# Starting the large on-chip buffers of a four-stage transformer layer at multiples of 128 bytes

## The reference, cut to what matters

```python
# 1  "cond": nine gated experts (eight weighted by gating probabilities, one shared), all on every token
out1 = (1 - sg) * sum_e g[e] * ((silu(x @ Wg[e]) * (x @ Wu[e])) @ Wd[e]) + sg * shared(x)     # 256 -> 1024 -> 256
# 2  "hyp": causal attention, 16 heads of 16, with hyperbolic distances as scores, then a projection
# 3  "cond2": two dense shared networks relu(x @ swi) @ swo, and one chosen by the sequence's type (5 types),
#            weighted by a small softmax gate
# 4  "ffn": layernorm, a 3-tap convolution, causal rotary attention, layernorm, a router (argmax over 4 experts)
#            and out = x + (silu(h @ wv_gate) * (h @ wv_value)) @ proj of the chosen expert, 256 -> 1024 -> 256
```

## The kernel before, in words

| stage | moving operand | loaded operand |
|---|---|---|
| cond up, B11, B21, B22, T1 | `cond_x_hi_first` 16512 (128) | `cond_w_hi` 123776 (128), `cond_w_lo` 152448 (128) |
| cond up, T2, T3, T4; remainders | `cond_x_hi` 82816 (128), `cond_x_lo` 95104 (128) | the same |
| cond down | `cond_h_hi` 197504 (128), `cond_h_lo` 205696 (128) | `cond_d_hi` 181120 (128), `cond_d_lo` 189312 (128) |
| hyp projection | `hyp_wq_hi` 64384 (128), `hyp_wq_lo` 70528 (128) | `hyp_src_hi` 152512 (192), `hyp_src_lo` 160704 (192) |
| dense up | `c_x_hi` 141728 (160), `c_x_lo` 158112 (160) | `dense_w_hi` 177696 (32), `dense_w_lo` 185888 (32) |
| dense down | `dense_h_hi` 210464 (32), `dense_h_lo` 218656 (32) | `dense_d_hi` 194080 (32), `dense_d_lo` 202272 (32) |
| typed up | `typed_x_hi` 158112 (160), `typed_x_lo` 162208 (160) | `typed_w_hi` 125344 (160), `typed_w_lo` 133536 (160) |
| rope projection | `rope_wq_hi` 221152 (224), `rope_wq_lo` 215008 (224) | `rope_src_hi` 156800 (128), `rope_src_lo` 164992 (128) |
| moe up | `moe_x_hi` 165152 (32), `moe_x_lo` 169248 (32) | `moe_w_hi` 116000 (32), `moe_w_lo` 132384 (32) |

## Time and profile before

### The profile page before, as it was taken

How to read it: one execution, slowest core, us unless ns; L and a number is a source line. 1 busy time by engine, 2 the same in 40 slices (tenths; PEclk the granted TensorE clock), 3 DMA queues, 4 the chain that set the end, 5 groups by cost and what they waited for, 6 DMA issues and landing times. The chain is left out here.

```text
span 2069.8 us, 35351 instructions
## 1 busy us (share of the span) xinstructions
PE 1923.5 (93%) x12240; PEld 1620.3 (78%) x12240; DVE 1434.9 (69%) x2398; ACT 1105.4 (53%) x2118; POOL 849.8 (41%) x854
## 2 busy tenths in 40 slices
PE   8999999999999999999998677999999768959998
PEld 6788888888888888888887465788799646849998
DVE  7777676767767676776776896433589577857776
ACT  6555555545555554555544697232355365636664
POOL 7350321405032140504200185220399225968885
PEclk9999999999999999999999799999999779969999
DMA  4101010010101001010102201310156215556661
GB/s 155 62 1 62 1 61 0 20 41 0 61 0 61 0 23 37 0 61 0 29 1 62 62 3 42 123 41 11 63 192 211 65 26 148 185 204 209 213 214 45
DMA packets 96322, 144.51 MB, mean 70 GB/s; under 512 B 15358, under 2 KB 72608, under 8 KB 96096
## 3 DMA queue, kind: packets, MB, share of 16 engines
q1 hardware_dynamic: 89168, 127.21, 19.1%
q0 software_dynamic: 4928, 12.86, 1.8%
q10 hardware_dynamic: 2128, 3.15, 0.4%
HBM read 111.46 MB, written 14.16 MB: 61 GB/s over the span
## 5 line engine op out<-in xcount | busy, mean ns | idle before, releaser
L319 PE MATMUL ps<-cond_x_lo,cond_w_hi 128*128 128x512 f32 x1008 | 392.6, 389 | 0.0
L471 ACT ACTIVATE cond_h_hi<-cond_h 128x512 fp32r<-128x512 f32 x288 | 174.0, 630 | 289.7 <-DVE cond_h L666 289.6
L805 POOL TENSOR_TENSOR cond_w_lo<-cond_stage_up,cond_w_hi 128x512 fp32r<-128x512 f32 x36 | 47.1, 1308 | 591.8 <-ACT cond_w_hi L471 591.8
L319 PE MATMUL ps<-cond_x_hi_first,cond_w_hi 128*128 128x512 f32 x578 | 230.1, 398 | 3.1 <-DVE ps L652 2.5
L382 PE MATMUL ps<-cond_h_hi,cond_d_hi 128*128 128x512 f32 x576 | 224.8, 390 | 4.1 <-DVE cond_h_lo L671 4.1
L319 PE MATMUL ps<-cond_x_hi_first,cond_w_lo 128*128 128x512 f32 x578 | 225.2, 390 | 0.0
L382 PE MATMUL ps<-cond_h_hi,cond_d_lo 128*128 128x512 f32 x576 | 224.3, 389 | 0.0
L382 PE MATMUL ps<-cond_h_lo,cond_d_hi 128*128 128x512 f32 x576 | 224.2, 389 | 0.0
L319 PEld LDWEIGHTS ps<-cond_x_lo,cond_w_hi 128*128 128x128 f32 x1008 | 189.3, 188 | 37.2
L649 DVE TENSOR_TENSOR ps<-cond_p_row,ps 128x512 f32<-128x512 f32 x142 | 98.7, 695 | 170.7 <-PE ps L319 170.7
L524 ACT ACTIVATE cond_h<-ps 128x512 f32<-128x512 f32 x216 | 124.7, 596 | 164.8 <-DVE cond_h_lo L671 132.2
(11 more groups left out here) (427 smaller groups left out, 5122.4 us busy)
## 6 DMA issues: line engine op xcount, KB each, us to landing
moe_stage_up<-in_L_ffn_expert_wv SPq DMA_DIRECT2D x22, 1024.0 KB, 7.9
typed_stage_up<-in_L_cond_wi SPq DMA_DIRECT2D x11, 1024.0 KB, 5.0
typed_stage_dn<-in_L_cond_wo SPq DMA_DIRECT2D x11, 1024.0 KB
moe_stage_dn<-in_L_ffn_expert_proj SPq DMA_DIRECT2D x11, 1024.0 KB
cond_stage_up<-in_L_cond_Wg SPq DMA_DIRECT2D x7, 1024.0 KB, 5.1
cond_stage_up<-in_L_cond_Wu SPq DMA_DIRECT2D x7, 1024.0 KB, 7.2
cond_stage_dn<-in_L_cond_Wd SPq DMA_DIRECT2D x7, 1024.0 KB, 9.5
rope_v_now<-rope_v_blk SPq DMA_DIRECT2D x16, 272.0 KB, 2.4
```

What stands on the lines that cost most here:

```text
L319: ins = pe.matmul(bank, ws[:, j, u, w], xs.rearrange("p o n -> p (o n)"), start=(opens and k == 0), stop=(k == 2), skip_group_check=True)
L471: copy = lambda dst, src: act.activation(dst, src, ACT.Copy)
L805: return pool.tensor_tensor(w_lo[:, j, :, A11:A12 + 1], raw_up[:, :, :, upper(j)], w_hi[:, j, :, A11:A12 + 1], ALU.subtract)
```

## The change

A helper `fill_line` allocates an unused buffer just large enough that the next buffer starts at a multiple of 128 bytes, and it is called ahead of the large buffers of each stage. `spike` and `space` are split over two lines for it, and in `rotary` the two buffers `v_now` and `yT` change places. No instruction is added, removed or moved; what differs is the addresses in them.

```diff
--- before.py
+++ after.py
@@ -28,6 +28,7 @@
 E_COND, E_TYPE, E_SHARED, E_MOE = 8, 5, 2, 4
 SLOT = 256
 HEAD = 2
+LINE = 128
 
 SLOTS = max((N + E_TYPE * (SLOT - T)) // SLOT, (N + E_MOE * (SLOT - 1)) // SLOT)
 LN_EPS = 1e-5
@@ -77,6 +78,13 @@
 
 def aligned(at):
     return (at + 31) // 32 * 32
+
+
+def fill_line(nc, ctx, side=None):
+
+    short = nc.sbuf_top % LINE if side else -aligned(nc.sbuf_base) % LINE
+    if short:
+        ctx.enter_context(nc.sbuf_tensor(f"fill_{aligned(nc.sbuf_base)}", [P, short // 4], F32, side=side))
 
 
 class StageSemaphores:
@@ -961,6 +969,7 @@
 
     with ExitStack() as s:
         sb = lambda name, shape, dt=F32: s.enter_context(nc.sbuf_tensor(f"{tag}_{name}", shape, dt))
+        fill_line(nc, s)
         w_hi = sb("w_hi", [P, ups, KC, F], F32R)
         w_lo = sb("w_lo", [P, ups, KC, F], F32R)
         d_hi = sb("d_hi", [P, FC, D], F32R)
@@ -1261,6 +1270,7 @@
         self.m, self.biased = m, b_qkv is not None
         if b_qkv is not None:
             self.bias, self.bo, self.ws = sb("bias", [P, 2 * D]), sb("bo", [P, KC]), sb("ws", [P, KC])
+            fill_line(nc, ctx, side)
             self.vb = sb("vb", [P, D])
             self.loads += [(self.bo[:], col(b_out)), (self.ws[:], col(w_sur)),
                            (self.vb[:], b_qkv[2 * D:].unsqueeze(0).to_broadcast([P, D]))]
@@ -1309,8 +1319,10 @@
         wide = lambda v: v.unsqueeze(0).to_broadcast([P, D])
         self.loads = [(self.w[:], wide(ln_w)), (self.b[:], wide(ln_b)), (self.wr[:], w_r.rearrange("(k p) e -> p k e", p=P))]
         self.loaded = ctx.enter_context(nc.semaphore("router_loaded"))
+        fill_line(nc, ctx)
         self.res, self.x = sb("res", [P, 2, KC, P]), sb("x", [P, 2, D])
         self.stats, self.mean, self.rstd = sb("stats", [P, 2, 6]), sb("mean", [P, 2, 2]), sb("rstd", [P, 2])
+        fill_line(nc, ctx)
         self.x2, self.xn, self.rows, self.hT = sb("x2", [P, 2, D]), sb("xn", [P, 2, D]), sb("rows", [P, 2, 2 * D]), sb("hT", [P, 2, KC, P])
         self.eps, self.logits = sb("eps", [P, 1]), sb("logits", [P, NP, E_MOE])
         self.best, self.free, self.hot = sb("best", [P, NP]), sb("free", [P, NP]), sb("hot", [P, NP, E_MOE])
@@ -1622,7 +1634,9 @@
         v_blk = sb("v_blk", [P, NP, 2, HP, 2, VW])
         wo = w.wo
         bias, bo, ws = w.bias, w.bo, w.ws
-        spike, space = sb("spike", [P, NP]), sb("space", [P, NP, 2 * H])
+        spike = sb("spike", [P, NP])
+        fill_line(nc, s)
+        space = sb("space", [P, NP, 2 * H])
 
         sem = StageSemaphores(nc, tag + "_in")
         src_rounded, src_ready = sem("src_rounded"), sem("src_ready")
@@ -1638,6 +1652,7 @@
             src_hi, src_lo = sb1("src_hi", [P, 2, KC, TW], F32R), sb1("src_lo", [P, 2, KC, TW], F32R)
             v_row, v_two = sb1("v_row", [P, 2, SUB, D]), sb1("v_two", [P, 2, SUB, 2, D])
             sig = sb1("sig", [P, NP])
+            fill_line(nc, s1)
             sq = sb1("sq", [P, 2, QK])
             r2, ln, root, inv, ep, en, sm, ser, below, cosh = (
                 sb1(n, [P, NP, 2 * H]) for n in ("r2", "ln", "root", "inv", "ep", "en", "sm", "ser", "below", "cosh"))
@@ -1907,13 +1922,14 @@
     chosen, last_steps, last_lifted = sem("chosen"), sem("last_steps"), sem("last_lifted")
     with ExitStack() as s:
         sb = lambda name, shape, dt=F32: s.enter_context(nc.sbuf_tensor(f"{tag}_{name}", shape, dt))
+        fill_line(nc, s)
         qk, v_blk = sb("qk", [P, NP, QK]), sb("v_blk", [P, NP, 2, HP, 2, VW])
         wo, wq_hi, wq_lo = w.wo, w.wq_hi, w.wq_lo
         hi_at = aligned(nc.sbuf_base)
         src_hi, src_lo = sb("src_hi", [P, 2, KC, TW], F32R), sb("src_lo", [P, 2, KC, TW], F32R)
         v_row, v_two = sb("v_row", [P, 2, SUB, D]), sb("v_two", [P, 2, SUB, 2, D])
         x32, rot = sb("x32", [P, 2, QK]), sb("rot", [P, 2, QK])
-        v_now, yT = sb("v_now", [P, 2, 2, HP, 2, VW]), sb("yT", [P, 2, KC, P])
+        yT, v_now = sb("yT", [P, 2, KC, P]), sb("v_now", [P, 2, 2, HP, 2, VW])
         mx, rec = sb("mx", [P, 2, H]), sb("rec", [P, 2, H])
 
         def placed(at, *parts):
@@ -2989,6 +3007,7 @@
     dn_half_done = sem("dn_half_done")
     with ExitStack() as s_:
         sb = lambda name, shape, dt=F32: s_.enter_context(nc.sbuf_tensor(f"{tag}_{name}", shape, dt))
+        fill_line(nc, s_)
         w_hi, w_lo = sb("w_hi", [P, ups, KC, F], F32R), sb("w_lo", [P, ups, KC, F], F32R)
         d_hi, d_lo = sb("d_hi", [P, FC, D], F32R), sb("d_lo", [P, FC, D], F32R)
         x_hi, x_lo = sb("x_hi", [P, 2, KC, SLOT], F32R), sb("x_lo", [P, 2, KC, SLOT], F32R)
@@ -3454,6 +3476,7 @@
                     ffn(nc, m, "dense", False, groups, None, [s0, s1], x_hi, x_lo, stage, SortBeside(lists, rows, slots))
                     sem.give_back()
                 brief = right.enter_context(ExitStack())
+                fill_line(nc, right, "right")
                 rope = AttentionWeights(nc, m, right, brief, "rope", a["L0_ffn_attn_w"], a["L0_ffn_proj_w"], side="right")
                 joining = JoinWeights(nc, brief, a["L0_cond2_g1"], a["L0_cond2_g2"], a["L0_ffn_ln1_w"], a["L0_ffn_ln1_b"],
                                       a["L0_ffn_conv_w"])
```

## The result

The changed kernel takes 2078.88 us (median of 5 runs, 2075.32 to 2079.67), the kernel before 2066.95 (5 runs beside them, 2065.03 to 2069.87): 11.9 us more, ratio 1.005, 95% interval 1.0039 to 1.0062. It is slower, as forecast, by three quarters of the 16 us that were forecast; 2083 lay 4 us above the measured time.

The account below looks back on a forecast made before the run. PE was taken to bound the kernel, its matmuls covering 93% of the span and all of cond; +17 us in cond and -0.6 in rope, +16 on the median 2066.95, gave 2083 us, range 2061 to 2091.

Parts of the forecast that it names:

- Reading (b): TensorE's pace depends on the distance by 256 between moving operand and weights; slower, 2083 us (2072 to 2091), chance 0.48.
- Reading (a): TensorE's pace depends on absolute starts: those that are not multiples of 128 cost time.
- rival 3: Stages outside cond get faster from multiples of 128: about 2063 us (chance 0.12) or 2045 (0.08), 0.20 together.
- Rival 2: No change: TensorE's pace doesn't depend on starts; 2067 us, 2064 to 2070, chance 0.32.
- rival 4: Cond's buffers were aligned already, so the change has no effect there; same time as no change, no chance of its own.
- The price of a disturbed matmul: Cond: 12 matmuls of each group of 33 slow to dense up's pace, +5.0 ns each, 60 ns a group.
- The price of healing: Cond: three matmuls behind each of three disturbed runs lose 6.6 ns each, 59 ns a group.
- The parts priced at nothing: Hyp, dense, typed, moe, ACT, POOL, DVE and DMA: 0 us each, some with small bounds.
- point ii: Sign in the profile after: dense up still at 232 ns between starts.
- point iv: Sign in the profile after: moe and typed at 120.0 ns between starts.
- Point (i): Sign: cond's settled matmuls at about 230 ns instead of 226.7, about 434 in 100 us, cond ending 15 us later.
- point iii: Rope's 512-column projection settles at 226.7 ns as its distance goes from 160 to 0; -0.6 us over 96 matmuls.

Follow-up runs that it names:

- i_cond_all128: Kernel before with 128 unused bytes between cond's token-side operands and its weights, putting all 21 up matmuls of a group at distance 128: 2085.93 us, ratio 1.0082.
- a_cond_shift: Kernel before with 128 unused bytes ahead of cond's own buffers, `cond_x_hi_first` not moved: 2079.02 us, ratio 1.0044.
- b_after_cond_back: Changed kernel with 128 more unused bytes ahead of cond's own buffers, bringing `cond_x_hi_first` back to distance 0: 2067.76 us, ratio 0.9992 to the kernel before.
- c_all_160: Kernel before with 160 unused bytes below everything, `cond_x_hi_first` included, no distance within a stage changed but rope's: 2070.66 us, ratio 1.0004.
- first scan: Kernel before with unused bytes ahead of dense weights (128), typed and moe token operands (128, 64) and hyp's source (192): 2064.28 us, ratio 0.9973.

## Why the prediction was right, and where its working was not

**The mechanism.** Reading (b) stands: the distance between the moving operand and the weights loaded beside it. Moving the loaded operand (`i_cond_all128`), or both but `cond_x_hi_first` (`a_cond_shift`), brings the loss; distance 0 at other absolute starts (`b_after_cond_back`, `c_all_160`) is free of it. Reading (a), rival 3, is out by the same two runs, and by dense, which the change aligned and left at 1.39 us for 6. Rival 2, no dependence on starts, and rival 4, that the change does nothing in cond, are out by `a_cond_shift`. Why a distance should matter is not settled by any run; that the two reads of TensorE meet in one part of the memory in some order that depends on it fits, but it is argued, not shown. The rule of the Trainium skill (SBUF — State Buffer, Who interferes with whom) that TensorE's two read ports are independent and that it waits on nobody does not hold for the pace here: moving one operand by 128 bytes against the other costs 107 ns in 33 matmuls, and by that rule it would cost nothing.

**The price of a disturbed matmul** (12 x 5.0 = 60 ns a group) was too high, by more than half. By medians against 226.7 ns each, the twelve matmuls of B11, T1, B21 and B22 lose 24 ns in sum: B11 and T1 16, B21 4, B22 4. Only eight of the twelve stream `cond_x_hi_first`; the `cond_x_lo` ones between them stand at distance 0, and the pace goes 234, 226, 234, 224 ns. Dense up, the row that I took, has all its matmuls at 128. Where all are, as in `i_cond_all128`, the price is even a little above the row: (2.80 / 12) = 233 ns, +6.6.

**The price of healing** (9 x 6.6 = 59 ns a group) was too low: the other 21 matmuls of a group have 82 ns over the pace: T2 14, the six down behind B21 29, T3 14, the six down behind it 25, T4 0. I let three matmuls heal after each run, as dense down's first three do. Here it takes the six behind B21 and has not ended when B22 comes, and nine behind B22 (3 of T3, 6 down). Together 24 + 82 = 106 ns, measured 107, priced 119: two errors that stood against each other, so that the group's price came near by luck.

**From the group to the kernel** was the step that made 17 us out of what became 8 to 12. 144 x 107 ns is 15.4 us. But the mean of the 142 groups rises only from 7601 to 7662 ns, and 144 x 61 ns is 8.8 us. The prediction had said that over these 1000 us the end moves by exactly what the pace moves, since PE is busy 100% of them. It is not free of waits: a gap of 0.1 us between two matmuls does not show in a busy share, because a matmul's modelled duration covers it. The waits between 120 and 1050 us (us in total, times, longest us), before and in the changed kernel:

```profile
PEld ps L319 <- DVE ps L652: 7.5, 24, 0.3
PEld ps L319 <- ACT cond_p_row L471: 4.1, 16, 0.3
...
PEld ps L327 <- DVE ps L660: 4.2, 16, 0.3
PEld ps L327 <- ACT cond_p_row L479: 1.1, 7, 0.2
```

PE waits there until DVE or ACT is done with a tile of `ps`, and a slower PE comes later and waits less: 11.6 us in 40 waits become 5.3 in 23. Matmul by matmul from 120 us on, the 70 places with more than 245 ns between starts in either kernel take 3.8 us less in sum, and all other places 11.9 us more, together the 8.1 us that cond loses from there. The 11.9 are less than 107 ns in each of the 130 groups, 13.9, since some matmuls were off the pace before: the place of the earlier trace rows stands right behind a wait (335 ns between the starts at 156.88 and 157.22), and nine matmuls behind such a wait run unsettled at distance 0 too. So the step that was mis-sized is the overlap: the prediction gave PE no wait in cond that could shrink. The same holds in `i_cond_all128`: 144 x 167 = 24 us by the median, 144 x 113 = 16.3 by the mean, 16.7 measured, with 1.9 us of waits left between 120 and 1050 us.

**The parts priced at nothing** were right: hyp (232.7 ns with 512 columns in the changed kernel, 233.2 before), dense (point ii), typed and moe (point iv), ACT, POOL, DVE, DMA. Point (i) was right in kind: 230.0 ns in a settled group, 436 matmuls in 100 us where 434 was said, cond ending 8.2 us later where 15 was said. **Rope** (point iii) was wrong in its step, though not in its price: at distance 0 it kept 231.1 ns on the mean, and its 96 matmuls won 96 x 2.1 = 0.2 us in place of 0.6. "The settled pace goes with distance 0" was inferred from stages of one width. With 512 and 256 columns in turns, in rope and in hyp of the first scan, distance 0 doesn't settle; at 256 columns 0 is the slow distance, which may be what unsettles the others, but no run separates the two. And for typed and moe I had called 120.0 ns "the settled pace": it is even, but it is the worst of the eight distances.

## What to carry to other kernels

Where TensorE is full, compare the starts of successive matmuls of equal shape between stages: where one is some nanoseconds off another, look at the addresses of the two operands that are read at the same time, relative to each other and by 256, before rounding anything to a line. With 128x512 float32 matmuls the distance 0 was best, with 256 columns 64 or 192; a kernel in which buffers of both kinds were placed by this won 0.4%, a part of it perhaps by the clock in rope, while one that rounded all to 128 bytes lost 0.5%. And price a change of pace by the mean of all places, not by the settled one, and look for short waits that a slower engine would no longer meet: a busy share of 100% hid 11.6 us of them here.

## What was not expected of the hardware

- At distance 0 the settled matmul takes 226.7 ns with 512 columns and 120.0 with 256. The difference, 106.7 ns for 256 columns, is one cycle of 2.4 GHz a column, and what is left over it is 13.3 ns at both widths. At 256 columns and distance 192 runs of twelve go at 113.3, half of 226.7, so that half of these 13.3 ns is gone.
- After the last matmul at distance 128 the pace of the next ones is off for six to nine matmuls and in a fixed pattern. Behind B22 it is 234, 229, 231, 231, 236, 228, 232, 231, 227 ns, by medians the same to the ns in the changed kernel and in `a_cond_shift`; behind the fifteen of `i_cond_all128` it is 230, 236, 228, 232, 231, 227. So it is no noise. A wait of PE of 0.1 us sets off such a run as well, with no distance but 0 near it: behind the one at 159.13 us before, 235, 233, 236, 224, 231, 236, 228, 233, 231 ns, then 226.
- A distance of 64 is as bad as 128 at 512 columns and among the best at 256.
- Absolute starts at remainder 0, 32, 64 or 128 made no difference to PE, ACT, DVE, POOL or the loads that any run could show.
